# A ring of one gather per tile of 128 edges, with PE reading each item's home from a register

## The reference, cut to what matters

```
x = x + _L0_gnn_ref(_layernorm(x), edge_index, ...)      # attention over the edges
x = x + _L0_ffn_ref(_layernorm(x)[None], ...)[0]         # 8 experts
x = x + _L1_gnn_ref(_layernorm(x), edge_index, W_l, W_r, b)
x = x + _L1_ffn_ref(_layernorm(x)[None], ...)[0]         # 64 experts, 2 of them per row

def _L1_gnn_ref(x, edge_index, W_l, W_r, b):
    src, dst = edge_index
    msg = x[src]
    agg = segment_sum(msg, dst, num_segments=n)
    deg = segment_sum(ones, dst, num_segments=n)
    mean = agg / maximum(deg, 1.0)[:, None]
    h = mean @ W_l + b + x @ W_r
    return h * sigmoid(h)
```

## Time and profile before

| what | value |
|---|---|
| median of 3 runs | 2432.34 us |
| span of the profiled execution, first to last instruction | 2427.9 us |
| mean granted TensorE clock | 0.936 |
| PE busy, share of the span | 2033.5 us, 84% |
| POOL busy, share of the span | 1037.0 us, 43% |
| L1139, 416 gathers | 393.5 us busy, 946 ns each |
| L1186, 832 matmuls (two for an item) | 395.9 us busy |

### The profile page before, as it was taken

One profiled execution on the slowest core, in us unless ns is written; L12 is line 12 of the kernel. 1 busy time (PEld: TensorE's weight loads), 2 busy tenths in 40 slices (PEclk: granted clock), 3 DMA queues, 4 the chain that ended last, 5 costly groups with the idle time before them and its releaser, 6 DMA issues. The chain is left out here.

```text
span 2427.9 us, 33639 instructions
## 1 busy us (share of the span) xinstructions
PE 2033.5 (84%) x8826; PEld 1296.0 (53%) x8826; DVE 1467.7 (60%) x3150; ACT 919.9 (38%) x2800; POOL 1037.0 (43%) x1073
## 2 busy tenths in 40 slices
PE   5957888888885726089999998998999999999998
PEld 4735666666664224033333333455445888888534
DVE  6647999999998661565555555587763222222343
ACT  2324565566663503455555555444101111111000
POOL 1147777777752305177777777400001111111331
PEclk9978999999997858589999999998899999999999
DMA  4558888888863535777777777775314999999652
GB/s 142 127 175 241 248 248 248 245 248 248 248 189 114 213 103 114 242 241 224 223 224 224 223 224 238 237 269 186 119 63 163 367 365 366 366 365 362 235 192 88
DMA packets 278021, 543.48 MB, mean 224 GB/s; under 512 B 44001, under 2 KB 122049, under 8 KB 277677
## 3 DMA queue, kind: packets, MB, share of 16 engines
q0 software_dynamic: 82592, 268.48, 37.9%
q1 hardware_dynamic: 177219, 240.65, 29.2%
q10 hardware_dynamic: 18058, 32.64, 3.9%
HBM read 455.87 MB, written 86.57 MB: 223 GB/s over the span
## 5 line engine op out<-in xcount | busy, mean ns | idle before, releaser
L895 PE MATMUL g_psA<-g_G,g_oh 128*128 128x261 f32 x1760 | 447.5, 401 | 88.8 <-DVE acc L1062 69.8
L832 POOL DMA_INDIRECT g_G<-tab,src_of_item x440 | 430.6, 979 | 171.8 <-issue 104.5
L1186 PE MATMUL g_psA<-g_G,g_oh 128*128 128x512 f32 x832 | 395.9, 610 | 96.7 <-DMA g_G<-tab,src_of_tile 64.8
L1139 POOL DMA_INDIRECT g_G<-tab,src_of_tile x416 | 393.5, 946 | 171.0 <-issue 78.9
L1225 DVE TENSOR_TENSOR acc<-acc,g_psA 128x512 f32 x416 | 285.6, 687 | 214.1 <-PE g_psA L1186 175.2
L895 PEld LDWEIGHTS g_psA<-g_G,g_oh 128*128 128x128 f32 x1760 | 328.4, 195 | 157.0 <-issue 91.9
L953 ACT ACTIVATE g_G<-g_G 128x64 f32<-128x64 f32 x1320 | 320.2, 335 | 0.0
L1186 PEld LDWEIGHTS g_psA<-g_G,g_oh 128*128 128x128 f32 x832 | 147.1, 191 | 323.3 <-issue 203.7
L2360 PE MATMUL mo_bank<-mo_xT,mo_w 128*128 128x128 f32 x2304 | 269.1, 275 | 0.2 <-ACT mo_xT L2397 0.2
L2360 PEld LDWEIGHTS mo_bank<-mo_xT,mo_w 128*128 128x128 f32 x2304 | 263.0, 192 | 1.0 <-ACT mo_xT L2397 0.5
L2263 POOL DMA_INDIRECT mo_g<-tab,mo_slot x72 | 68.0, 945 | 457.1 <-PE mo_bank L2350 325.1
(11 more groups left out here) (420 smaller groups left out, 2554.7 us busy)
## 6 DMA issues: line engine op xcount, KB each, us to landing
mo_w<-in_L_ffn_w SPq DMA_DIRECT2D x216, 512.0 KB, 8.0
ys<-mo_y ACTq DMA_DIRECT2D x72, 256.0 KB, 5.7
g_ot<-reld SPq DMA_DIRECT2D x26, 512.0 KB, 6.1
ys<-sg_zeros SPq DMA_DIRECT2D x24, 512.0 KB, 3.9
g_G<-tab,src_of_item POOLq DMA_INDIRECT x440
g_pen<-pend SPq DMA_DIRECT2D x208, 32.0 KB
g_G<-tab,src_of_tile POOLq DMA_INDIRECT x416, 3.7
tab<-fi_row SPq DMA_DIRECT2D x25, 261.0 KB, 2.6
```

The costliest lines, as they stand in the source:

```text
L832: q.indirect_dma_start(G[:, j % RING, :], None, tab0, bass.IndirectOffsetOnAxis(K.src[:, j:j + 1], 0)).then_inc(gs[g % 3], 16)
L895: ins = tens.matmul(psA[u][:, f, 0:HW], oh[:, n % OR, h, :], G[:, r + h, f * HW:(f + 1) * HW], start=(h == 0), stop=(h == SUP - 1))
L1139: g.indirect_dma_start(G[:, n % MR, :], None, table, bass.IndirectOffsetOnAxis(K.src1[:, n:n + 1], 0)).then_inc(got[n % MR], 16)
L1186: tens.matmul(psA[n % MB][:], oh[:, n % MO, :], G[:, n % MR, :], start=True, stop=True).then_inc(summed, 1)
```

## The change

A tile is gathered once, so there are 392 gathers, into a ring of 32 places: tile j has its home at place j mod 32. The items stay 416. Since an item's tile depends on the data, PE reads two numbers for each item from SBUF into registers: the tile's number plus one (`til1`), which it compares with the count of landed tiles, and the tile's place in the ring (`slot1`), from which the matmul's address is made. PE reads item n+1's two numbers before item n's waits. The count `landed` is kept by SP, which waits for each tile's own semaphore in order and increments one common semaphore. Gather j waits until `summed` has reached j - 7, since of the tile that was at this place before, the last item may be 24 items further on. The rings of one-hots shrink from 8 to 6 and from 4 to 3; `W_r`, its bias and the turned rows move into SBUF that the next phase will use; SP's two weight loads now stand behind the last tile's landing. In `phase_first` the source rows come by one plain DMA instead of four indirect ones, and DVE makes the two lists.

```diff
@@ phase_first, tile_list
                     v.wait_ge(blocks1, 1)
+                    ch(vv.tensor_tensor(tilf[:], irow[:], psY[0:1, 0:NIT1], ALU.subtract))
                     vv.tensor_copy(K.blk1[:], psY[0:1, 0:NIT1]).then_inc(blkread1, 1)
-                    v.wait_ge(got1, LQ * 2 * 16)
+                    vv.tensor_copy(K.til1[:], tilf[:])
+                    ch(vv.tensor_scalar(tili[:], tilf[:], -1.0, None, ALU.add))
+                    vv.tensor_single_scalar(K.slot1[:], tili[:], MR - 1, ALU.bitwise_and)
+                    v.wait_ge(srcl, 16)
+                    vv.tensor_copy(sf1[:], si1[:])
+                    v.wait_ge(got1, LQ * 16)
                     ch(vv.tensor_copy(df1[:], di1[:]))
...
-MR = 20
-MO = 8
+MR = 32
+MO = 6
 MB = 4
-MT = 4
+MT = 3
...
@@ phase_mean, POOL
-            for n in range(NIT1):
-                wait(g, summed, n - MR + 1)
-                g.indirect_dma_start(G[:, n % MR, :], None, table,
-                                     bass.IndirectOffsetOnAxis(K.src1[:, n:n + 1], 0)).then_inc(got[n % MR], 16)
+            for j in range(NET):
+                wait(g, summed, j - MR + NX + 1)
+                g.indirect_dma_start(G[:, j % MR, :], None, table,
+                                     bass.IndirectOffsetOnAxis(K.src1[:, j:j + 1], 0)).then_inc(got[j % MR], 16)
@@ phase_mean, SP
+            own_load(0)
+            own_load(1)
+            for j in range(NET):
+                s.wait_ge(got[j % MR], (j // MR) * 16 + 16)
+                s.sem_inc(landed, 1)
+                i, r = divmod(j - 10, OWN_AT)
+                if r == 0 and 0 <= i < NT - 2:
+                    own_load(i + 2)
             s.dma_start(s2[:], a["L1_gnn_W_l"].rearrange("(k p) d -> p k d", p=P)).then_inc(early, 16)
             s.dma_start(s13[0:E1, 0, 0, :], a["L1_ffn_gate_w"]).then_inc(early, 16)
@@ phase_mean, PE
-            def item(n):
+            def home(n):
+                return (t.value_load(K.til1[0:1, n:n + 1], min_val=1, max_val=NET),
+                        t.value_load(K.slot1[0:1, n:n + 1], min_val=0, max_val=MR - 1))
+
+            def item(n, tile1, slot):
                 t.wait_ge(ready, n + 1)
-                t.wait_ge(got[n % MR], (n // MR) * 16 + 16)
+                t.wait_ge(landed, tile1)
                 wait(t, added, n - MB + 1)
-                tens.matmul(psA[n % MB][:], oh[:, n % MO, :], G[:, n % MR, :], start=True, stop=True).then_inc(summed, 1)
+                tens.matmul(psA[n % MB][:], oh[:, n % MO, :], G[:, ds(slot, 1), :].rearrange("p o d -> p (o d)"),
+                            start=True, stop=True).then_inc(summed, 1)
...
+            at = home(0)
             for n in range(NIT1):
-                item(n)
+                ahead = home(n + 1) if n + 1 < NIT1 else None
+                item(n, *at)
+                at = ahead
```

More of the change, by code:

```diff
@@ L240, in build @@
         K.part = sb("part", [P, 1])
[L241 to L244, removed]
+        K.src1 = sb("src_of_tile", [P, NET], I32)
+        K.til1 = sb("tile_of_item", [1, NIT1], I32)
+        K.slot1 = sb("slot_of_item", [1, NIT1], I32)
         K.nrel1 = sb("negrel_of_tile", [P, NIT1])
@@ L247, in build @@
         K.rdeg = sb("rdeg", [P, NT, 1])
-        K.a3 = sb("a3", [P, NT, 3, H0], BF16)
-        with nc.sbuf_tensor("acc", [P, NT, RW], F32) as acc:
+        with (nc.sbuf_tensor("src_of_item", [P, NIT * SUP], I32) as K.src,
+              nc.sbuf_tensor("rel_of_item", [P, NIT * SUP], F32) as K.rel,
+              nc.sbuf_tensor("blk_of_item", [1, NIT], I32) as K.blk,
+              nc.sbuf_tensor("a3", [P, NT, 3, H0], BF16) as K.a3,
+              nc.sbuf_tensor("acc", [P, NT, RW], F32) as acc):
             phase_first(nc, K, a, tab0, esrc, edst, reld, pend, pqd, acc)
@@ L287, in phase_first @@
     WHOLE = (NSUP - 1) * SUP * P
-    assert 2 * NI2 == NIT and NI2 <= P and LQ * NI4 == NIT1
+    NS4 = NET // LQ
+    assert 2 * NI2 == NIT and NI2 <= P and LQ * NI4 == NIT1 and LQ * NS4 == NET
     with Phase(nc, "fi") as p:
@@ L314, in phase_first @@
         pb1 = p.sb("pb1", [NI4, LQ])
-        di1 = p.sb("di1", [NI4, LQ, 2, P], I32)
-        df1 = p.sb("df1", [NI4, LQ, 2, P])
+        di1 = p.sb("di1", [NI4, LQ, P], I32)
+        df1 = p.sb("df1", [NI4, LQ, P])
+        si1 = p.sb("si1", [NS4, LQ, P], I32)
+        sf1 = p.sb("sf1", [NS4, LQ, P])
+        irow = p.sb("irow", [1, NIT1])
+        tilf = p.sb("tilf", [1, NIT1])
+        tili = p.sb("tili", [1, NIT1], I32)
         nr1 = p.sb("nr1", [NI4, LQ, P])
@@ L362, in phase_first @@
         got1 = p.gather_sem("got1")
+        srcl = p.sem("srcl")
         reldone1 = p.sem("reldone1")
@@ L392, in _ @@
                            allow_small_or_imprecise_dtypes=True).then_inc(firsts, 1)
+            nc.gpsimd.iota(irow[:], [[1, NIT1]], base=1, channel_multiplier=0,
+                           allow_small_or_imprecise_dtypes=True).then_inc(firsts, 1)
             nc.gpsimd.iota(K.iota[:], [[1, P]], base=0, channel_multiplier=0,
@@ L407, in _ @@
             for q in range(LQ):
[L408 to L411, removed]
+                g.indirect_dma_start(di1[:, q, :], None, edst[1].rearrange("s (h e) -> (s h) e", h=SUP),
+                                     bass.IndirectOffsetOnAxis(cnti1[:, q:q + 1], 0)).then_inc(got1, 16)
+            g.wait_ge(got1, LQ * 16)
         @b.sync
@@ L466, in _ @@
                             .rearrange("s o -> o s")).then_inc(lastb, 16)
+            c.dma_start(si1[:], esrc.rearrange("s (h e) -> (s h) e", h=SUP)
+                        .rearrange("(q p) e -> p q e", q=LQ)).then_inc(srcl, 16)
             for n in range(NT + 2):
@@ L567, in levels_of @@
                 v.wait_ge(lastb, 16)
-                v.wait_ge(firsts, 6)
+                v.wait_ge(firsts, 7)
                 ch(vv.tensor_single_scalar(b1i[:], b1i[:], 7, ALU.arith_shift_right))
@@ L662, in tile_list @@
                     for q in range(LQ):
-                        ins = vv.tensor_scalar(nr1[:, q], df1[:, q, 1], -1.0, pb1[:, q:q + 1], ALU.mult, ALU.add)
+                        ins = vv.tensor_scalar(nr1[:, q], df1[:, q, :], -1.0, pb1[:, q:q + 1], ALU.mult, ALU.add)
                     ins.then_inc(reldone1, 1)
@@ L666, in tile_list @@
                     v.wait_ge(itemt1, 1)
-                    vv.tensor_copy(K.src1[:], psX[:, 0:NIT1])
+                    vv.tensor_copy(K.src1[:], psX[:, 0:NET])
                     vv.tensor_copy(K.nrel1[:], psY[:, 0:NIT1])
@@ L1092, in _ @@
             v.wait_ge(added, NIT)
-MR = 20
-MO = 8
+MR = 32
+MO = 6
 MB = 4
-MT = 4
+MT = 3
 OWN_AT = NIT1 // NT
+assert MR & (MR - 1) == 0 and MR > NX
 def phase_mean(nc, K, table, acc, a, own, s13, s2):
@@ L1107, in phase_mean @@
         far = p.sb("far", [P, MT, P])
-        wr = p.sb("wr", [P, KT, D])
-        bb = p.sb("bb", [P, D])
+        wr = s13[:, 1]
+        bb = s13[:, 0, 3, :]
         xr = p.sb("xr", [P, 2, D])
-        xrT = p.sb("xrT", [P, 2, D])
+        xrT = s13[:, 0, 1:3, :]
         psA = [p.ps(f"psA{u}", [P, D]) for u in range(MB)]
@@ L1115, in phase_mean @@
         got = [p.gather_sem(f"got{q}") for q in range(MR)]
+        landed = p.sem("landed")
         apart = p.sem("apart")
@@ L1136, in _, with own_load @@
         def _(g):
-            for n in range(NIT1):
-                wait(g, summed, n - MR + 1)
-                g.indirect_dma_start(G[:, n % MR, :], None, table,
-                                     bass.IndirectOffsetOnAxis(K.src1[:, n:n + 1], 0)).then_inc(got[n % MR], 16)
+            for j in range(NET):
+                wait(g, summed, j - MR + NX + 1)
+                g.indirect_dma_start(G[:, j % MR, :], None, table,
+                                     bass.IndirectOffsetOnAxis(K.src1[:, j:j + 1], 0)).then_inc(got[j % MR], 16)
         @b.sync
         def _(s):
-            s.dma_start(wr[:], a["L1_gnn_W_r"].rearrange("(k p) d -> p k d", p=P)).then_inc(wl, 16)
-            s.dma_start(bb[:], a["L1_gnn_b"].partition_broadcast(P)).then_inc(wl, 16)
-            for i in range(NT):
+            s.dma_start(wr, a["L1_gnn_W_r"].rearrange("(k p) d -> p k d", p=P)).then_inc(wl, 16)
+            s.dma_start(bb, a["L1_gnn_b"].partition_broadcast(P)).then_inc(wl, 16)
+            def own_load(i):
                 wait(s, turned, i - 1)
                 s.dma_start(xr[:, i % 2, :], table[i * P:(i + 1) * P, :]).then_inc(xl[i % 2], 16)
+            own_load(0)
[6 more added lines that the diff above has]
+                    own_load(i + 2)
             s.dma_start(s2[:], a["L1_gnn_W_l"].rearrange("(k p) d -> p k d", p=P)).then_inc(early, 16)
@@ L1228, in keep @@
                 v.wait_ge(prod, i + 1)
-                vv.tensor_tensor(own[:, i, :], psP[i % 2][:], bb[:], ALU.add).then_inc(kept, 1)
+                vv.tensor_tensor(own[:, i, :], psP[i % 2][:], bb, ALU.add).then_inc(kept, 1)
             v.wait_ge(wl, 32)
```

2 lines of the change are left out of this document (1 added, 1 removed).

## The result

The changed kernel takes 2561.45 us (median of 4 runs, 2556.04 to 2568.45) against 2432.19 us for the kernel before in the same comparison. The ratio is 1.0531, 95% interval [1.0503, 1.0559]: slower by 5.3%. The forecast was 2557 (2500 to 2630).

The account below looks back on a forecast made before the run. POOL's gathers, one per 1.251 us, were taken to bound the second aggregation; after the change PE's queue would, adding 123 us. With 2 us for `phase_first`, the span of 2427.9 became 2553, plus 4.4 around it: 2557 us, range 2500 to 2630.

Parts of the forecast that it names:

- The bar of 0.125 us an item: Second aggregation: PE has 52 us to spare, 0.125 us an item; any more added to its path makes PE set the phase.
- "nothing" for SP, ACT and the rings: Part three: SP's relay and moved weight loads, ACT, DVE and the smaller one-hot rings add no time.
- 1.51 us an item: PE's queue in the second aggregation: two loads, address, matrix instructions and three waits take 1.51 us, bounds 1.42 to 1.60.
- the unpriced wait on a register's value: PE's semaphore wait on a loaded value might be dearer; no row shows it; 0.1 us more would add 42 us.
- First item: Start of the second aggregation: four register loads come before item 0 and delay it by 2.7 us, to 1044.4.
- `phase_first`: DVE's making of the lists lengthens one step: plus 2 us, bounds 0 and 3; four fewer indirect DMAs are worth nothing.
- A: Rival: PE's register work is hidden and POOL stays the bound in the second aggregation, so faster, 2414 us; 5%.
- B: Rival: an item's two loads overlap on PE's queue, 1.21 us an item, 2434 us; 3%.
- C: Rival: PE's clock falls in the second aggregation, a phase of 717 us, 80 over the forecast, 2637 us; 10%.
- the 42 us: Cost of the change if a TENSOR_LOAD took the skill page's 200 ns, with an item at 1.31 us.

Follow-up runs that it names:

- e4: Changed kernel with one register load an item: tile not read, item waits for landing n + 1 (at most 392); ratio 0.9998 to the kernel before.
- e9: Changed kernel with one checked load an item, home worked out by remainder, SP's two late weight loads issued earlier; 2406.2 us, ratio 0.9897 to the kernel before.
- e7: Changed kernel with tile and slot read by one load of two registers, the slot's check left out; ratio 0.9922 to the kernel before.
- e1: Kernel before plus one unused checked register load on PE for each item of the second aggregation; ratio 1.0005.
- e2: Kernel before plus two unused checked register loads on PE for each item of the second aggregation; ratio 1.0352.
- e3: Kernel before plus three unused checked register loads on PE for each item of the second aggregation; one run, 2776.5 us (before: 2425.0).
- e10: As e9, but SP's two weight loads stay behind the landing of gather 392, as in the changed kernel; ratio 0.9896 to the kernel before.
- e6: Changed kernel with tile and slot read by one load of two registers, both bounds checked, three checks an item; ratio 1.0641 to the kernel before.

## Why the prediction was right

**The mechanism, by its steps.** That POOL sets the phase before, at 1.251 us, is shown by e4 and e9, where its pace is the same with 24 gathers fewer. The bar of 0.125 us an item for what may be added to PE's path does not hold for work of the queue: e7's items come 1.12 us apart between products, 0.26 over the array's 0.86, and its phase, with the 24 gathers fewer, is still 17 us shorter than before. The prediction's sum did not use that bar, but took the longest of the queue's, the array's and POOL's time. That rule is right on both sides of the crossing: e1 (0.78 us of queue: free), and the changed kernel. Near the crossing it gives too little: for e7 the queue's sum is 416 x 1.12 + 9 = 475 us and POOL's 490, but PE's items take 497.6 us (1047.1 to 1544.7), so near the crossing the queue's time and the array's add up in part. That a load holds the queue for 0.65 us is measured: 0.638 from e2 to e3. The pair e1 and e2 shows that the delay of a load is hidden and its throughput isn't. e4 shows "nothing" for SP, ACT and the rings, in a phase that POOL sets.

**The terms.** For loads, address and waits 1.51 us an item were forecast. Between products 1.53 are measured, so 0.02 more, and from the first item's weight load (1046.84) to the last item's (1692.19) 645.4 us, where 636 were forecast. The address and the wait on a register are what the changed kernel has beyond e2: (656.9 - 611.1) / 415 = 0.110 us, where 0.09 was in the sum for the address alone. So the unpriced wait on a register's value costs 0.02 us or less. The trace shows where the 0.02 are. PE's queue has one record an item for waits, at line 96 (both shown here stand in 1402.6 to 1406):

```profile
L96 PEldq EVENT_SEMAPHORE  x2: 51/51/51, 1403.3 to 1404.8; - x2
```

By starts in narrowed windows, an item's two loads begin at 1403.53 and 1404.17, the record of the waits at 1404.81, the address at 1404.94, and the next load at 1405.07. So the loads hold the queue for 0.64 us each (0.65 forecast), the waits for 0.11 to 0.14 (0.09), and the address with four matrix instructions for 0.13 (0.13). The waits are the term that was too small.

First item: +2.7 us were forecast, but it starts 8.6 us after POOL's first gather against 8.2 before, since the register loads (from 1044.0) ran while the first landing was still awaited, which SP's relay passed on at 1045.9. The two errors have opposite signs, and together they give 130.9 us for the phase where 123 were forecast. Over the whole kernel +125 us were forecast; the medians give +129, the pair of profiles +133. Runs of the changed kernel lie up to 12 us apart, so that the total came within 5 us is in part luck, and the terms say more. The 4.4 us taken to lie around the span are a median less another execution's span; within one run it is 1.7 to 1.9 us in all of this record.

**`phase_first`.** I took +2 us, and the profile after seems to say +5.0. The other runs say that this is scatter: `phase_gat` starts at 149.58, 150.16, 150.26 and 149.72 in before and e1 to e3, and at 154.58, 149.50, 147.38, 152.55, 150.44, 149.13, 150.39 and 153.04 in the eight kernels with the change's lists (in e9 and e10 without the slots). The means are 149.9 and 150.9, with a spread of 7 us in the second group. One profile can't give this term; 1 us, with an uncertainty that takes in 0 and 2, is all that can be said.

**The rivals.** A (queue work hidden) is refuted by the result and e2. It is true where the queue's time is under the array's or near it: e1, e4, e9 (loads 0.91 us apart in its queue). Its time for a kernel bound by POOL, 2414, is near e7's 2412 by luck: there the queue's lag ends the phase, and the 12.4 us for SP's weights in it were too many (e10). B (loads overlap) is refuted by 1.53 us and by the slope of e3; the two loads of an item stand 0.64 us apart. C did not come about in the changed kernel: from 1052.6 to the phase's end the granted clock is 1.00, with PE busy 65.6 of 80 us and a pause in each item. With a third load (e3) the clock does fall, to a mean of 0.90 in the stretch shown, so this rival was nearer than it looks.

Two readings of rows in the prediction were too smooth. The two stretches of the earlier trace rows are alike to 1.5% for PE and POOL, but DVE and ACT differ by 4%. And the present phase was not at 1.00 throughout: the clock was 0.50 until 1045.0 and again from 1488.8 to 1499.0, where PE had just waited 3.65 us. Neither moves the sum.

The Trainium skill, "Runtime: NRT & Kernel Launch", section on instruction fetch mechanics, gives about 200 ns for a register, for registers that the runtime loads from HBM. The loads here read SBUF, one register at a time, and take 302 ns each, 0.64 us with the check. So the 42 us that the prediction worked out from the page's figure (an estimate) is a third of what was measured.

## What to carry to other kernels

Price register work on an engine as the queue time of a loop body, and compare it with the engine's own time for that body: well below it, it is free; above it, each load costs its full 0.65 us; near it, some of it shows (e7). Count a checked load as two parts of about equal price, the read (0.36 us) and the check (0.29 us); read one value and work the other out of it, instead of two reads or one read of two registers. A saving on the engine that sets the pace is worth something only while no other engine, its queue included, comes within that saving.

## What the runs showed that I had not expected

- A bounds check costs nearly as much as the read (0.29 of 0.65 us), though its records show 0.16 us of work.
- A TENSOR_LOAD goes by the register: 0.302 us for one, 0.544 for two.
- Two checks with different bounds on one value add up: e6 has three per item for two values, and is slower by 24 us than two separate loads.
- A remainder in an address costs 0.04 us, seven times less than the check.
- The start of `phase_gat` scatters by 7 us between executions of kernels whose `phase_first` is nearly alike, so that a 2 us term can't be read from one pair of profiles.
- With three loads an item the clock fell again and again, though PE never idled longer than 1.2 us; with two it stayed at 1.00.
